# Output projection in one block with attention, its first weights and half tile prepared during the last pair of sequences

## The reference

```python
scores = jnp.where(valid[:, None, None, :], scores, -1e+30)
probs = jax.nn.softmax(scores, axis=-1)
o = jnp.einsum('bhqk,bkhd->bqhd', probs, v_all)      # 64 sequences, 32 heads, 544 keys, head size 128
o = o.reshape(bsz, seqlen, HQ * D)                   # 32 * 128 = 4096
return jnp.einsum('bse,de->bsd', o, Wo)              # to 512, then x = x + this
```

## Time and profile before

| | |
|---|---|
| median of three runs | 2530.89 us (2530.7 to 2532.8) |
| the profiled execution | 2538.01 us |
| its span in the profile | 2536.5 us |
| TensorE busy | 2426.7 us, 96% |
| VectorE, ScalarE, GpSimd busy | 71%, 63%, 25% |
| attention's last matmul, projection's first | 2139.33 us, 2161.36 us |

### The profile page before, as it was taken

How to read it: one execution, slowest core, us unless ns; L and a number is a source line. 1 busy time by engine, 2 the same in 40 slices (tenths; PEclk the granted TensorE clock), 3 DMA queues, 4 the chain that set the end, 5 groups by cost and what they waited for, 6 DMA issues and landing times. The chain is left out here.

```text
span 2536.5 us, 55776 instructions
## 1 busy us (share of the span) xinstructions
PE 2426.7 (96%) x16326; PEld 2209.0 (87%) x16327; DVE 1802.9 (71%) x3697; ACT 1589.4 (63%) x3317; POOL 641.9 (25%) x932
## 2 busy tenths in 40 slices
PE   6799899999999979999999999999999997699999
PEld 4688688888888769999999999999999997588887
DVE  5455345999998878888888888888888884544443
ACT  3222236877777768888888888888888884311111
POOL 1222130000000034444444444444444442000000
PEclk9899899999999989999999999999999999899999
DMA  6522332333333478888888898888888874766664
GB/s 223 158 69 80 132 141 88 101 117 101 100 99 108 118 224 286 292 294 299 286 295 301 282 303 294 287 302 283 296 301 283 302 267 167 271 201 218 210 214 148
DMA packets 376132, 541.47 MB, mean 213 GB/s; under 512 B 49394, under 2 KB 263090, under 8 KB 372210
## 3 DMA queue, kind: packets, MB, share of 16 engines
q1 hardware_dynamic: 303922, 316.33, 39.2%
q0 software_dynamic: 70016, 221.30, 25.3%
q10 hardware_dynamic: 2112, 2.89, 0.4%
HBM read 442.06 MB, written 98.30 MB: 213 GB/s over the span
## 5 line engine op out<-in xcount | busy, mean ns | idle before, releaser
L1632 PE MATMUL both_ps_o<-att_pt,att_v 128*128 128x128 f32 x4096 | 540.2, 275 | 0.0
L1331 ACT ACTIVATE att_prob<-att_prob,att_shift 128x544 f32<-128x544 f32 x512 | 384.1, 750 | 209.5 <-DVE att_shift L1355 197.7
L1632 PEld LDWEIGHTS both_ps_o<-att_pt,att_v 128*128 128x128 f32 x4096 | 504.8, 191 | 0.0
L1355 DVE CUSTOM_DVE_ANT_0 att_prob<-both_ps_s,att_mask 128x544 f32<-128x544 f32 x512 | 366.1, 715 | 0.0
L1326 DVE TENSOR_TENSOR att_k_lo<-att_k_raw,att_k_hi 128x1024 fp32r<-128x1024 f32 (+1 forms) x320 | 338.4, 1057 | 1.9 <-ACT att_k_hi L1319 1.9
L101 PE MATMUL both_ps_s<-att_k_hi,att_q_hi 128*128 128x272 f32 x1024 | 339.1, 331 | 0.5 <-DVE att_k_lo L1326 0.5
L1609 PE MATMUL both_ps_pt<-both_ident,att_prob 128*128 128x128 f32 x2048 | 309.5, 274 | 5.9 <-ACT att_prob L1331 4.3
L103 PE MATMUL both_ps_s<-att_k_hi,att_q_lo 128*128 128x272 f32 x1024 | 297.9, 291 | 0.0
L1511 ACT ACTIVATE att_pt<-both_ps_pt 128x512 f32<-128x512 f32 x512 | 294.9, 576 | 2.4 <-PE both_ps_s L1617 1.2
L102 PE MATMUL both_ps_s<-att_k_lo,att_q_hi 128*128 128x272 f32 x1024 | 295.1, 288 | 0.0
L1319 ACT ACTIVATE att_k_hi<-att_k_raw 128x1024 fp32r<-128x1024 f32 (+1 forms) x320 | 292.8, 915 | 0.0
(11 more groups left out here) (196 smaller groups left out, 5171.3 us busy)
## 6 DMA issues: line engine op xcount, KB each, us to landing
att_k_raw<-in_k_pages SPq DMA_DIRECT2D x1024, 128.0 KB, 5.2
q_t<-qkv_out_t SPq DMA_DIRECT2D x128, 256.0 KB, 2.3
att_q_raw<-q_t POOLq DMA_DIRECT2D x64, 512.0 KB, 7.4
o_t<-att_o POOLq DMA_DIRECT2D x64, 512.0 KB, 6.8
out_o<-o_t SPq DMA_DIRECT2D x32, 1024.0 KB, 6.6
out_inv<-inv_t SPq DMA_DIRECT2D x32, 1024.0 KB, 6.7
qkv_w_stage<-in_w_qkv SPq DMA_DIRECT2D x12, 1024.0 KB, 5.1
l_w_stage<-in_w SPq DMA_DIRECT2D x8, 1024.0 KB, 7.4
```

The source lines that it names most:

```text
L1331: act.activation(prob[:, b, :], prob[:, b, :], ACT.Exp, bias=shift[:, b:b + 1], scale=-1.0, accum_out=total[:, j // HK, j % HK:j % HK + 1] ...
L1355: dve.tensor_tensor_reduce(out=prob[:, b, :].rearrange("p (a n) -> p a n", a=2), in0=ps_s[:, j % 2, :, 0:HALF], in1=mask[:, j // HK, :].re ...
L1632: pe.matmul(out, v_sb[p][:, c, h * DH:(h + 1) * DH], pt_sb[:, j % OG, c, :], start=(c == 0), stop=False)
```

## The change

The projection moves into the block of attention. Its weight groups are of two heads now (16 groups of 0.5 MiB). The raw weights lie where their low parts will be written, and each group's buffers lie where attention has no more use for what was there (raw keys, split keys, values, masks, probabilities, outputs); attention's own buffer `pt` moves up to make room. SP goes on from attention's page loads to the projection's loads, with waits on attention's counts. During the last pair ScalarE and VectorE get, unit by unit, the splits of groups 0 to 5 (high) and 0 to 4 (low), and the scale, high and low part of half tile 0 in units 12, 13 and 14. The wait for the last stores moves from POOL to SP and to ScalarE ahead of the high part of half tile 1. The semaphores `lo_done`, `s_done`, `masked`, `pv_done` and `zeroed` are shared. The helper `load_o` and `load_inv`, `split_w_lo`, `add` and the steady loops do what they did. The diff, cut to its core (empty lines left out):

```diff
+AFTER_O = AFTER_TAIL + 16384
+OUT_AT = (4 * (NSEQ * NPP + NKEY + 2 * NSEQ + NSEQ * NPP // PPP + 2 * NPP // PPP),
+          4 * ((NPP + 1) * HK * PSIZE + HK * P), 4 * 2 * HK * (NALL + P))
...
     rest.reach(AFTER_TAIL)
-    o_sb, pt_sb = rest.sb("o", [P, 2, HK, P]), rest.sb("pt", [P, OG, NKEY // P, P])
+    o_sb = rest.sb("o", [P, 2, HK, P])
     p_own, pto_sb, inv_sb = rest.sb("p_own", [P, 2, OG, SEQ]), rest.sb("pto", [P, 2, P]), rest.sb("inv", [HK, 2, P])
     vo_sb = [vo0, rest.sb("vo1", [P, HK // OG, OG, DH])]
+    rest.reach(AFTER_O)
+    pt_sb = rest.sb("pt", [P, OG, NKEY // P, P])
     v_sb = [v0, rest.sb("v1", [P, NPP // PPP, HK * DH])]
...
         in_pairs(pool, NSEQ // 2, pair)
         store(NSEQ - 1, 1)
-        for p in range(2):
-            pool.wait_ge(o_stored[p], 16 * NSEQ // 2)
-            pool.wait_ge(inv_stored[p], 16 * NSEQ // 2)
...
                 copy_pt(u, j)
+                if last:
+                    output.scalar(act, j)
...
+                if last:
+                    output.vector(dve, j)
...
+OUT_WG = 2
+OUT_GROUPS = HQ // OUT_WG
+OUT_HI = {6: 0, 7: 1, 9: 2, 10: 3, 14: 4, 15: 5}
+OUT_LO = {7: 0, 8: 1, 10: 2, 11: 3, 15: 4}
+OUT_SCALE, OUT_SPLIT_HI, OUT_SPLIT_LO = 12, 13, 14
+def output_projection(nc, m, place, both, pool_sems, x_in, o_t, inv_t, w, x_out):
+    HH = HQ // 2
+    WG, GROUPS, LOADS = OUT_WG, OUT_GROUPS, 4
+    PIECES_IN, UNITS_IN = PIECES * NSEQ, HK * NSEQ
+    _, _, _, o_stored, inv_stored = pool_sems
+    lo_done, s_done, masked, pv_done = both.lo_done, both.s_done, both.masked, both.pv_done
+    first, rest = place
+    w_raw, w_hi, w_lo = [], [], []
+    def weights(at, groups):
+        for g in groups:
+            w_hi.append(at.sb(f"w_hi{g}", [P, WG, D], fp32r))
+            here = at.at
+            w_lo.append(at.sb(f"w_lo{g}", [P, WG, D], fp32r))
+            w_raw.append(nc.alloc_sbuf_tensor_at(f"out_w{g}", [P, WG, D], fp32, offset=here))
+    AFTER_PAGES, AFTER_RAW, AFTER_KEYS = OUT_AT
+    first.reach(AFTER_PAGES)
+    weights(first, (0, 1))
+    first.reach(AFTER_PAGES + AFTER_RAW)
+    weights(first, range(2, 7))
+    o_0, inv_sb = rest.sb("o0", [P, SPT, HH, SEQ]), rest.sb("inv", [P, SPT, HH * SEQ])
+    x_sb, y_sb = rest.sb("x", [P, D]), rest.sb("y", [P, D])
+    rest.reach(AFTER_RAW)
+    weights(rest, range(7, 12))
+    rest.reach(AFTER_RAW + AFTER_KEYS)
+    oh_0, ol_0 = rest.sb("o_hi0", [P, HH, P], fp32r), rest.sb("o_lo0", [P, HH, P], fp32r)
+    o_1 = rest.sb("o1", [P, SPT, HH, SEQ])
+    late = Region(nc, "out", rest.at + 256)
+    rest.reach(AFTER_TAIL)
+    oh_1, ol_1 = rest.sb("o_hi1", [P, HH, P], fp32r), rest.sb("o_lo1", [P, HH, P], fp32r)
+    weights(rest, (12, 13, 14))
+    weights(late, (15,))
+    o_sb, oh_sb, ol_sb = [o_0, o_1], [oh_0, oh_1], [ol_0, ol_1]
+    ps_y = both.ps_s[:, 0, :, :]
...
+    def split_w_hi(act, g):
+        act.wait_ge(w_loaded[g % LOADS], 16 * (g // LOADS + 1))
+        act.activation(w_hi[g][:, :, :], w_raw[g][:, :, :], ACT.Copy).then_inc(w_hi_done, 1)
...
+    def split_hi(act, n, t, p):
+        act.wait_ge(scaled, n + 1)
+        if later(n, 2):
+            act.wait_ge(half_done, n - 1)
+        act.activation(oh_sb[p][:, :, :].rearrange("p h (s q) -> p s h q", s=SPT),
+                       o_sb[p][:, :, :, :], ACT.Copy).then_inc(hi_done, 1)
+    def scale(dve, n, t, p):
+        dve.wait_ge(o_loaded[p], 16 * (t + 1))
+        dve.wait_ge(inv_loaded, 16 * (n + 1))
+        o = o_sb[p][:, :, :, :].rearrange("p s h q -> p s (h q)")
+        dve.tensor_tensor(o, o, inv_sb[:, :, :], ALU.mult).then_inc(scaled, 1)
+    def split_lo(dve, n, p):
+        dve.wait_ge(hi_done, n + 1)
+        dve.tensor_tensor(ol_sb[p][:, :, :].rearrange("p h (s q) -> p s h q", s=SPT), o_sb[p][:, :, :, :],
+                          f32(oh_sb[p][:, :, :]).rearrange("p h (s q) -> p s h q", s=SPT),
+                          ALU.subtract).then_inc(split_done, 1)
+    def scalar_ahead(act, j):
+        if j in OUT_HI:
+            split_w_hi(act, OUT_HI[j])
+        if j == OUT_SPLIT_HI:
+            act.wait_ge(pv_done, UNITS_IN - HK)
+            split_hi(act, 0, 0, 0)
+    def vector_ahead(dve, j):
+        if j in OUT_LO:
+            split_w_lo(dve, OUT_LO[j])
+        if j == OUT_SCALE:
+            scale(dve, 0, 0, 0)
+        if j == OUT_SPLIT_LO:
+            split_lo(dve, 0, 0)
+    def sync(sp):
...
+        def load_w(g):
+            if g >= LOADS:
+                sp.wait_ge(w_split, g - LOADS + 1)
+            sp.dma_start(w_raw[g][:, :, :], w[g]).then_inc(w_loaded[g % LOADS], 16)
+        sp.wait_ge(lo_done, PIECES_IN - PIECES)
+        load_w(0)
+        load_w(1)
+        sp.wait_ge(s_done, UNITS_IN - HK)
+        load_w(2)
+        load_w(3)
+        sp.wait_ge(lo_done, PIECES_IN)
+        for p in range(2):
+            sp.wait_ge(o_stored[p], 16 * SPT // 2)
+            sp.wait_ge(inv_stored[p], 16 * SPT // 2)
+        load_o(0, 0)
+        load_inv(0, 0)
+        for g in range(4, 7):
+            load_w(g)
+        sp.wait_ge(s_done, UNITS_IN)
+        load_w(7)
+        sp.wait_ge(pv_done, UNITS_IN - HK)
+        sp.wait_ge(masked, UNITS_IN)
+        load_o(0, 1)
+        sp.wait_ge(scaled, 1)
+        load_inv(0, 1)
+        for g in range(8, 12):
+            load_w(g)
+        sp.wait_ge(pv_done, UNITS_IN)
+        for g in range(12, GROUPS):
+            load_w(g)
+        sp.dma_start(x_sb[:, :], x_in[0:P, :]).then_inc(x_loaded, 16)
+        for p in range(2):
+            sp.wait_ge(o_stored[p], 16 * NSEQ // 2)
+            sp.wait_ge(inv_stored[p], 16 * NSEQ // 2)
+        def pair(i, last):
+            for p in range(2):
+                t = 2 * i + p
+                if not (last and p):
+                    for half in range(2):
+                        sp.wait_ge(split_done, 2 * t + half + 1)
+                        load_o(t + 1, half)
+                        sp.wait_ge(scaled, 2 * t + half + 2)
+                        load_inv(t + 1, half)
...
+    def scalar(act):
+        for g in range(len(OUT_HI), GROUPS):
+            if g == GROUPS // 2 + 1:
+                act.wait_ge(pv_done, UNITS_IN)
+                for p in range(2):
+                    act.wait_ge(o_stored[p], 16 * NSEQ // 2)
+                    act.wait_ge(inv_stored[p], 16 * NSEQ // 2)
+                split_hi(act, 1, 0, 1)
+            split_w_hi(act, g)
+        def pair(i, last):
+            for j in range(4):
+                if later(i, 1) or j >= 2:
+                    split_hi(act, 4 * i + j, 2 * i + j // 2, j % 2)
+        in_pairs(act, NT // 2, pair)
+    def vector(dve):
...
+        for g in range(len(OUT_LO), GROUPS):
+            if g == GROUPS // 2:
+                scale(dve, 1, 0, 1)
+            if g == GROUPS // 2 + 1:
+                split_lo(dve, 1, 1)
+            split_w_lo(dve, g)
+        def pair(i, last):
+            for p in range(2):
+                t = 2 * i + p
+                if not (last and p):
+                    scale(dve, 2 * t + 2, t + 1, 0)
+                    split_lo(dve, 2 * t + 2, 0)
+                add(t, p)
+                if not (last and p):
+                    scale(dve, 2 * t + 3, t + 1, 1)
+                    split_lo(dve, 2 * t + 3, 1)
+        in_pairs(dve, NT // 2, pair)
+    def tensor(pe):
+        pe.wait_ge(masked, UNITS_IN - 1)
+        def pair(i, last):
+            for p in range(2):
+                t = 2 * i + p
+                if later(t, 2):
+                    pe.wait_ge(y_ready, t - 1)
+                for half in range(2):
+                    pe.wait_ge(split_done, 2 * t + half + 1)
+                    for h in range(HH):
+                        n = half * HH + h
+                        if not later(t, 1) and h % WG == 0:
+                            pe.wait_ge(w_split, n // WG + 1)
+                        mm = three_pass(pe, ps_y[:, p, :], oh_sb[half][:, h, :], ol_sb[half][:, h, :],
+                                        w_hi[n // WG][:, n % WG, :], w_lo[n // WG][:, n % WG, :],
+                                        half == 0 and h == 0, half == 1 and h == HH - 1)
+                    mm.then_inc(half_done, 1)
+        in_pairs(pe, NT // 2, pair)
+    return Ahead(None, scalar_ahead, vector_ahead, None), Programs(sync, None, scalar, vector, tensor)
...
+        out_ahead, out = output_projection(nc, Mem(nc, ctx, "out"), place("out"), both, pool_sems, x_in, o_t, inv_t, wo, x_out)
...
+                out.sync(sp)
...
+                out.scalar(act)
...
+                out.vector(dve)
...
+                out.tensor(pe)
...
-        "wo": a["L3_cond_Wo"].T.reshape(8, HQ // 8, DH, D).transpose(0, 2, 1, 3),
+        "wo": a["L3_cond_Wo"].T.reshape(OUT_GROUPS, OUT_WG, DH, D).transpose(0, 2, 1, 3),
```

More of the change, by code:

```diff
@@ L828, in qkv @@
     eps_sb = rest.sb("eps", [P, 1])
-    zeroed = m.sem("zeroed")
+    zeroed = both.zeroed
     x_loaded, xt_done, xhi_done, xt_split = m.sems("x_loaded", XB), m.sem("xt_done"), m.sem("xhi_done"), m.sem("xt_split")
```

(10 more changed lines are left out.)

195 lines of the change are left out of this document (43 added, 152 removed).

## The result

The changed kernel takes 2513.65 us, the median of four runs (2512.6 to 2516.0); the kernel before, repeated beside it, took 2531.66 (2530.7 to 2532.8). The ratio is 0.9925 with a 95% interval of 0.9912 to 0.9937: 18 us faster. Forecast were 2501.9 us and a range of 2494 to 2510. The direction was right, and some 11 us of the gain did not come.

The account below looks back on a forecast made before the run. The prediction took pauses and low clock between attention and projection, some 43 us, as the bound; the third half tile moves from 2204.92 to 2175.9, 29.0 us, so 2530.9 - 29.0 = 2501.9 us, range 2494 to 2510.

Parts of the forecast that it names:

- Part 1: Border between attention and projection: waits, first loads, scaling and splitting removed, alone worth up to 43 us.
- Part 2: Cost of the added work in attention's last pair: attention ends 4.7 us later than before.
- held copy: Last pair, VectorE: own-key probabilities' copy (line 1550) queued behind low parts; TensorE stands still 3.1 us before unit 12's last matmuls.
- The landing of o and inverse: Half tile 0's two 1 MiB loads in the last pair: issued about 2112.6, landed about 2127.5, with 1.5 us of slack.
- rival B: Last pair has no room: o and inverse land 4 to 6 us after 2129; gain 23 to 25 us; chance 0.13.
- Part 3: From attention's end to the third half tile: it starts at 2175.9 instead of 2204.92, 29.0 us earlier.
- half 2: Third half tile of the projection (tile 1, half 0); its split sets the kernel's end, forecast at 2175.9 us.
- rival C: No wait at the third half tile, tile 1's loads not behind the weights: gain 38 us, 2493 us; chance 0.04.
- The 328.3 us behind it: Projection from the third half tile's start at 2204.92 us to the end, claimed not to change.
- Part 4: Sizes without a row: 0.5 MiB weight load taken as 3.7 us; moving pt and sharing semaphores 0 us.
- A: Rival, last pair: line 1550's copy isn't held, TensorE ends attention at 2139.7; gain 33.7, 2497 us; chance 0.12.
- D: Rival, slower than before: VectorE stands at unit 12's scale for late loads, from 29 us late; chance 0.03 with the like.

Follow-up runs that it names:

- own_copy_first: Changed kernel with VectorE's copy of the own-key probabilities made before the low parts of half tile 0 and group 4; 2605.01 us, 0.9902 of the kernel before.
- hold_456: Changed kernel with the loads of weight groups 4 to 6 held back until the first inverse has landed; 2608.15 us, 0.9912 of the kernel before.
- all_four: Changed kernel with the edits of all_three plus that of hold_456; 2503.26 us, 0.9873 of the kernel before.
- all_three: Changed kernel with the edits of weights_64_on, tile1_first and own_copy_first together; 2499.24 us, 0.9858 of the kernel before.
- after_again: The changed kernel unedited, run again on another chip, slower for every kernel; 2607.18 us, 0.9922 of the kernel before.
- tile1_first: Changed kernel with tile 1's first loads of o and inverse issued ahead of weight groups 12 to 15; 2509.69 us, 0.9897 of the kernel before.
- weights_64_on: Changed kernel with weight groups 0 to 6 starting 64 bytes later in every partition, no instruction changed; 2505.61 us, 0.9889 of the kernel before.

## Why the prediction was right or wrong

**Part 1 (the removed border): right.** The projection's first matmul comes 0.14 us after attention's last; the next idle time is 0.56 us.

**Part 2 (the last pair): the held copy right, the landing and the low clock too small.** The units 6 to 11, costed at nothing, cost nothing: the mask of unit 14 ends 17.2 us after the mark in both kernels. The held copy is there with the releaser that was named, and own_copy_first shows it. Three terms were off:
- The landing of o and inverse. The step "some 5.3 MB at 389 GB/s is 14 us", with its 1.5 us of slack, failed: 6.7 MB went through in 18.3 us, at 368 GB/s. The 5.3 MB were 1 MiB of weights, 2 of o and inverse and 2 of values. Left out were the 0.5 MiB store of o that POOL issues at 2111.56, ahead of the inverse's landing, some 1.0 MB of the weight groups 4 to 6, and most of the time at a load's start and end, for which Part 3 takes 2.9 us in the same kind of sum. hold_456 and all_four leave out groups 4 to 6 and gain little: 0.7 us in all_four against all_three, nothing in hold_456 against after_again. Their 5.7 MB (5.3 and the store) go through in some 15 us, and the rest of the 17.5 is the end in which the engines are nearly idle. How much the store and the values on the other queue cost, no run took apart, nor what the end consists of. VectorE stood for 2.52 us. That is the beginning of rival B, at half its size.
- This lateness made a second pause, 1.37 us, before the transposes of unit 15, because the mask of unit 15 stands behind the scale; and the copy's pause was 3.63 us, forecast 3.1.
- The low clock behind the pause: 1.6 us forecast by the row of the 3.57 us pause, 2.8 measured (6.4 us from line 1641's first matmul to the end, 3.6 at full clock). The low level lasted 5.9 us from the end of the pause, against 3.4 behind the 3.57 us pause of before.

Attention thus ends 8.2 us later than before instead of 4.7. The prediction had named a pause in attention ahead of unit 12's last matmuls as a sign of being wrong, and the pause of 1.37 us is one.

**Part 3 (from attention's end to half 2): right.** Counted from the projection's first matmul, half 2 was forecast 31.5 us later and came 32.1 us later. Its wait was forecast at 9.7 us and was 8.8, the landing of the inverse at 9.4 us from its issue and was 9.57, and the step that VectorE's row of low parts sets the issue of group 15 held. ScalarE's wait for the last store cost nothing. Nor was that store late: POOL issued it in 0.56 us at 2144.31, while VectorE ran the low parts of groups 5 to 7 (2143.93 to 2147.42). The prediction took the Trainium skill's rule on two-input instructions (SBUF — State Buffer, Who interferes with whom) to mean that it would wait for these. The rule speaks of GpSimd instructions that read SBUF, and the same section reports no stall of DMA beside `tensor_tensor`; the trace agrees with that, and the row was right to go by. tile1_first shows that the rest of this pause is not to be had by order alone, and so rival C's price of 9.0 us (38 against 29) was too high: its loads gave 2.5, since they cost the weights half of what they saved.

**"The 328.3 us behind it are 30 half tiles of 48 matmuls at 10.9 us each and do not change": wrong, the largest single term.** 14 half tiles of the 29 behind the third took 11.18 us instead of 10.88, 0.30 us more each, 4.2 us; half tiles of more than 11 us were among the prediction's own signs of being wrong. The instructions are the same; the places of their operands are not. The prediction had asked what each instruction costs and how many there are. Where its operands start it had taken for nothing, and in Part 4, too, moving a buffer was put at 0. Without these 4.2 us the median would be 2509.4, just inside the range that was stated; weights_64_on is the kernel in which they are gone.

**Part 4.** The 0.5 MiB weight load: 4.8 us median behind 2080 us, 3.7 taken, 2.7 and 5.0 the bounds. It was of no weight for the sum, as said. The Trainium skill's advice (DMA: Bandwidth & Descriptors, Bandwidth) of at least 1 MiB a transfer had no test here; with 0.5 and 1 MiB transfers mixed the engines were at 0.98 to 1.07 of their time and moved 311 to 402 GB/s, against 389 at 1.01 before, and no run tells the two sizes apart. The attention pace did not change, so moving `pt` did cost 0.

**The median.** The forecast subtracted from the median, and this was sound: the 4.7 us by which the mark lay earlier in this pair of profiles would otherwise have counted as gain.

**Rivals.** A (the copy not held) did not occur, and was then built: own_copy_first, worth 2.6 us behind the mark where A was priced at 4.7. B occurred in part. C did not occur, and its order of loads was built as tile1_first. D did not: the landing took 18.3 us, not 45. What the range lacked was a case for the steady part; it was drawn from the border alone.

## What to carry to other kernels

When buffers move, compare the steady matmul spacing (matmuls started in 100 busy us) of the two profiles before explaining anything else, and place the two operands of a long row of matmuls at equal starts modulo 256 bytes; here this cost or gave 4.2 us for seven of sixteen groups, and 9.3 us where all were unequal. Work put into an engine's idle time belongs behind the small copies that another engine waits for in the same unit. A load in a stretch that was idle before is reckoned with all bytes that are under way there, the stores too, and with its start and end; and holding back what stands behind it brought 0.7 us at most here and cost 3.2 in the end.

## What the hardware showed unexpectedly

- A 128x512 matmul follows the last one after 226.7 ns where the starts of the stationary and the moving operand are equal modulo 256 bytes, and after 233.3 ns where they are not, at clock 1.00 in both. The ten rows of the table, from seven kernels, agree. At the low clock level the spacing in half 2 is 427 ns in both kernels, before (equal starts) and after (unequal).
- Two pauses of nearly the same length, 3.57 and 3.63 us, were followed by the low clock level for some 3.4 and 5.9 us. A pause of 2.82 us between attention's last units (after_again) cost 1.6 us of low clock as well, and the pause of 2.13 us in all_three none. What decides the length stayed open.
- The inverse of half tile 0 took from 17.2 us (after_again) to 19.0 us (own_copy_first) from issue to use in the nine profiles of kernels with the changed order of loads, where the median of such a load had been 7.1; the DMA share was 0.98 to 1.07 meanwhile in the changed kernel. In hold_456 the engines were 11% busy in the last 2.2 us before it landed.
